# Gate and up of two of four batches by seven products of quarters

## The reference

```python
x = _layernorm(x + attention(x, Wqkv, bqkv, Wo, bo))          # 16 heads of 32
x = _layernorm(x + _wkv(w, u, x, ctx))                        # recurrence over the 512 tokens, per channel
Wg, Wu, Wd = dequant(gate_w), dequant(up_w), dequant(down_w)  # (w - 128) * scale per row; 2048x512, 2048x512, 512x2048
x = _layernorm(x + (silu(x @ Wg.T) * (x @ Wu.T)) @ Wd.T)
```

## Time and profile before

| | us |
|---|---|
| median of 3 runs (lowest, highest) | 726.25 (724.97, 728.55) |
| the profiled execution: its own time | 728.07 |
| its span, first to last instruction | 726.0 |
| busy: PE / DVE / ACT / POOL | 707.3 / 510.8 / 409.0 / 303.2 |

### The profile page before, as it was taken

One profiled execution on the slowest core, in us unless ns is written; L12 is line 12 of the kernel. 1 busy time (PEld: TensorE's weight loads), 2 busy tenths in 40 slices (PEclk: granted clock), 3 DMA queues, 4 the chain that ended last, 5 costly groups with the idle time before them and its releaser, 6 DMA issues.

```text
span 726.0 us, 11976 instructions
## 1 busy us (share of the span) xinstructions
PE 707.3 (97%) x4274; PEld 391.4 (54%) x4274; DVE 510.8 (70%) x1191; ACT 409.0 (56%) x980; POOL 303.2 (42%) x338
## 2 busy tenths in 40 slices
PE   8898999999999999998999999999999999999997
PEld 3466665666665666666554445445544444544445
DVE  3588766799899889899826889866787734532224
ACT  5478877769886787679755662154612532133310
POOL 2016421464766314541356834474645733023310
PEclk9999999999999999999999999999999999999999
DMA  7728739344233234643044010000001000100001
GB/s 230 227 87 212 241 73 242 86 123 117 66 92 115 51 104 130 143 76 88 3 63 112 1 59 15 30 16 1 0 16 44 0 1 1 43 16 1 0 15 44
DMA packets 45530, 54.16 MB, mean 75 GB/s; under 512 B 4896, under 2 KB 34848, under 8 KB 45472
## 3 DMA queue, kind: packets, MB, share of 16 engines
q1 hardware_dynamic: 41632, 46.59, 21.9%
q0 software_dynamic: 3264, 6.29, 5.1%
q10 hardware_dynamic: 576, 0.52, 0.3%
HBM read 47.10 MB, written 12.58 MB: 82 GB/s over the span
## 4 chain that ended last, share of the span: by engine, by line
PE 87%; DVE 4%; ACT 3%; DMA 2%; issue 2%; SPq 1%; POOL 1%; ACTq 0%; POOLq 0%; DVEq 0%
PE psb L838 29%; PE psb L726 10%; PE psb L764 8%; PE psb L862 7%; PE psb L860 7%; PE psb L742 6%; PE psb L809 5%; PE psb L777 5%; PE psb L753 4%; PE psb L825 2%; PE psb L797 2%; PE psb L788 2%; DMA ks<-parts 1%; ACT ee L949 1%; DVE st L1143 1%
## 5 line engine op out<-in xcount | busy, mean ns | idle before, releaser
L1098 DVE CUSTOM_DVE_ANT_0 ee<-psb,mask,clip 128x512 f32<-128x512 f32 (+3 forms) x256 | 130.6, 535 | 20.7 <-PE psb L753 20.1
L949 ACT ACTIVATE ee<-ee,nm 128x512 f32<-128x512 f32 (+3 forms) x256 | 142.0, 559 | 1.5 <-DVE nm L1098 1.5
L1433 POOL TENSOR_TENSOR hl<-hf,hh 128x512 f16<-128x512 f32 x64 | 74.2, 1160 | 103.6 <-ACT hh L1024 103.6
L1024 ACT ACTIVATE hh<-hf 128x512 bf16<-128x512 f32 x64 | 40.3, 630 | 119.6 <-DVE hf L1222 115.1
L960 ACT ACTIVATE ee<-psb 128x256 f32<-128x256 f32 (+1 forms) x156 | 81.5, 531 | 42.7 <-PE psb L764 36.3
L764 PE MATMUL psb<-ident,ee 128*128 128x128 f32 x640 | 98.9, 274 | 3.3 <-DVE ee L1112 1.5
L1222 DVE SCALAR_TENSOR_TENSOR hf<-th,c,psb 128x512 f32<-128x512 f32 x60 | 43.7, 729 | 79.8 <-PE psb L838 63.2
L838 PE MATMUL psb<-x2h,wg 128*128 128x512 f16 x256 | 97.0, 379 | 0.0
L838 PE MATMUL psb<-x2h,wu 128*128 128x512 f16 x256 | 97.0, 379 | 0.0
L838 PE MATMUL psb<-x2l,wg 128*128 128x512 f16 x256 | 97.0, 379 | 0.0
L838 PE MATMUL psb<-x2l,wu 128*128 128x512 f16 x256 | 97.0, 379 | 0.0
(11 more groups left out here) (130 smaller groups left out, 1215.7 us busy)
## 6 DMA issues: line engine op xcount, KB each, us to landing
qs<-parts SPq DMA_DIRECT2D x64, 128.0 KB, 2.9
ks<-parts SPq DMA_DIRECT2D x60, 128.0 KB, 3.4
parts<-qhl SPq DMA_DIRECT2D x16, 256.0 KB, 2.1
parts<-khl SPq DMA_DIRECT2D x16, 256.0 KB, 2.3
x<-in_x SPq DMA_DIRECT2D x4, 1024.0 KB, 6.9
ct<-in_ctxT SPq DMA_DIRECT2D x4, 1024.0 KB, 5.3
out<-x SPq DMA_DIRECT2D x16, 256.0 KB, 2.0
xt<-in_xT SPq DMA_DIRECT2D x14, 256.0 KB, 4.2
```

The costliest lines, as they stand in the source:

```text
L949: e.activation(dst, dst, ACT.Exp, bias=NM[:, n % 4, col:col + 1], scale=-1.0, accum_out=DEN[:, n % 4, col:col + 1]).then_inc(sem("exp"), 1)
L1098: e.tensor_tensor_reduce(E[H % 3][:, EOFF[i]:EOFF[i] + w], PSB[:, bank["score", H, i], 0:w], MASK[:, S - w:S], -SC, CLIP[:, i:i + 1], ALU. ...
L1433: e.tensor_tensor(HS[it][1][:], ring(b, it)[1][:], HS[it][0][:], ALU.subtract).then_inc(sem("hl"), 1)
```

## The change

Gate and up of a batch are one product of two by two blocks: rows gate and up, channels in halves, tokens in halves. For batches 2 and 3 (`SEVEN`) its eight block products become seven products of sums (the scheme of Strassen and Winograd). A pair m is two hidden tiles, 2m and 2m+1; a product P1 to P7 is 8 matmuls of 256 columns, (2 tiles) x (2 tiles of channels) x (high, low). What goes into it are blocks or sums of blocks of the weights (`WSUM`, four sums of two pieces each, made once) and of the tokens (`x_sum`, made per batch).

- PE, pair m: P1, P5, P2, P6, P3, P4 of pair m-1, P7. P6, P4 and P7 add on to the bank sa that holds P1; P3 adds on to the bank of P5. P6 waits for ScalarE's copy snap1 of P1, P3 for snap5 of P5, P7 for snap6 of P1+P6, P4 for c22.
- VectorE: c11 and c12 write the two token halves of gate to SBUF, c22 the second half of up; hfa and hfb are the two halves of hf, for each tile. The order is c11(m), c12(m), hfa(m-1) twice, c22(m), hfb(m) twice.
- ScalarE: snap1, snap5, snap6, two Silu (in SBUF, behind c12), two hh of pair m-1. GpSimd: two hl as before. `WS_POOL`, `HFB_POOL` and `XLO_POOL` are all zero, so all sums are VectorE's.
- Ahead of a batch: x2t is copied whole (xf), VectorE makes four token sums (xt, 512 columns each), ScalarE four high parts (xhi) and VectorE four low parts (xlo), of 1024, 1024, 1024 and 512 columns.
- The eight weight sums (128x2048, f16) stand at slots 272 to 295.
- The recurrence of batch 3 is placed at 280, 289, 291, 296 (before: 288, 292, 294, 297), its yt at 301, 301, 304, 306 (302, 303, 303, 308), its x2t at 312 (314). Batch 2's x2t stand at 292 (290, 291, 291, 292). Nearly all other slots, of attention too, and the tables `TURN`, `OH_POOL`, `XH_POOL`, `COPIES`, `KEYS` are set anew; of these only a few are shown.

```diff
-W_SPLIT = (6, 7, 8, 11)
+W_SPLIT = (8, 9, 18, 20)
...
-WKV_AT = {(0, 0): 111, (0, 1): 123, (0, 2): 133, (0, 3): 143, (1, 0): 191, (1, 1): 209, (1, 2): 262, (1, 3): 264,
-          (2, 0): 266, (2, 1): 272, (2, 2): 274, (2, 3): 277, (3, 0): 288, (3, 1): 292, (3, 2): 294, (3, 3): 297}
-YT_AT = {0: (156, 164, 174, 183), 1: (269, 270, 270, 270), 2: (283, 283, 286, 287), 3: (302, 303, 303, 308)}
-X2_AT = {0: (225, 228, 230, 232), 1: (272, 272, 272, 273), 2: (290, 291, 291, 292), 3: (314, 314, 314, 314)}
+WKV_AT = {(0, 0): 111, (0, 1): 123, (0, 2): 134, (0, 3): 144, (1, 0): 193, (1, 1): 208, (1, 2): 262, (1, 3): 264,
+          (2, 0): 266, (2, 1): 272, (2, 2): 274, (2, 3): 277, (3, 0): 280, (3, 1): 289, (3, 2): 291, (3, 3): 296}
+YT_AT = {0: (158, 166, 167, 182), 1: (268, 269, 270, 270), 2: (283, 286, 287, 288), 3: (301, 301, 304, 306)}
+X2_AT = {0: (225, 226, 228, 230), 1: (272, 272, 272, 273), 2: (292, 292, 292, 292), 3: (312, 312, 312, 312)}
+WS_AT = {1: (272, 280), 2: (280, 284), 3: (277, 295), 4: (285, 291)}
...
+    def quarters(b, c):
+        add("xf", b, c)
+        if c == T - 1:
+            for k in range(4):
+                add("xhi", b, 0) if k == 0 else None
+                add("xt", b, k)
+                add("xhi", b, k) if k else None
+            for k in range(4):
+                add("xlo", b, k)
...
+    def seven_first(b, m):
+        if m == 0:
+            tt.flush(("xlo", b, 3))
+        for j, name in ((1, "sa"), (5, "sd"), (2, "sb"), (6, None)):
...
+            add("p", b, m, j)
+            if j == 2:
+                add("c11", b, m)
+            else:
+                add(f"snap{j}", b, m)
+
+    def seven_second(b, m):
+        for j in (3, 4, 7) if m < PAIRS - 1 else (4, 7, 3):
+            if j == 4:
+                fourth(b, m - 1)
+                continue
+            add("p", b, m, j)
+            if j == 3:
...
+                add("c12", b, m)
+            else:
+                add("c22", b, m)
+        for it in (2 * m, 2 * m + 1):
+            add("silu", b, it)
+        for it in (2 * m - 2, 2 * m - 1) if m else ():
+            add("hh", b, it)
+            add("hl", b, it)
+        for it in (2 * m, 2 * m + 1):
+            add("hfb", b, it)
...
-            gu(b, it)
+            if b in SEVEN:
+                (seven_second if it % 2 else seven_first)(b, it // 2)
+            else:
+                gu(b, it)
...
+        def product(b, m, j):
...
+            for k in (0, 1):
+                for kk in (0, 1):
+                    for low in (0, 1):
+                        mm = e.matmul(PSB[:, bk, k * HALF_S:(k + 1) * HALF_S], weights(j, kk, 2 * m + k),
+                                      moving(b, j, kk, low), start=(unit is not None and k + kk + low == 0),
+                                      stop=(kk + low == 2), skip_group_check=True)
+            mm.then_inc(sem("p"), 1)
...
+        def c12(b, m):
+            dve.wait_ge(*by_p(b, m, 3))
+            dve.wait_ge(*by("snap6", b, m))
+            e.tensor_tensor(pair(b, m)[:, :, HALF_S:S], PSB[:, bank["sd", b, m], :].rearrange("p (k n) -> p k n", k=2),
+                            SNAP2.rearrange("p (k n) -> p k n", k=2), ALU.add).then_inc(sem("summed"), 1)
```

More of the change, by code:

```diff
@@ L20 @@
 EPS = 1e-5
+HALF_S = S // 2
 EOFF = {0: 0, 1: 128, 2: 384, 3: 768}
@@ L44 @@
 OHS = 6
+SEVEN = (2, 3)
+PAIRS = IT // 2
+SIGNAL = {"snap1": "snap", "snap5": "snap", "snap6": "snap", "c11": "summed", "c12": "summed", "c22": "summed"}
+PART_READ = {1: 1, 2: 0, 3: 0, 4: 3, 5: 1, 6: 2, 7: 2}
 EARLY = 4
-W_SPLIT = (6, 7, 8, 11)
[L50 to L53, removed]
@@ L61 @@
 LAST_AT = (5, 5, 6)
[L62 to L68, removed]
@@ L79 @@
-X2_AT = {0: (225, 228, 230, 232), 1: (272, 272, 272, 273), 2: (290, 291, 291, 292), 3: (314, 314, 314, 314)}
[L80 to L90, removed]
+WAIT = {'high': 1, 'low': 1, 'vtake': 1, 'r1': 2, 'norm': 6, 'exp': 4, 'eb': 0, 't1': 1, 't3': 0, 'oh': 3, 'ol': 3,
+        'ek': 1, 'scan_q': 2, 'scan_p': 6, 'divide': 8, 'r2': 3, 'x2h': 1, 'x2l': 2, 'expand': 0}
@@ new lines @@
+WAIT_IN = {'r1': 0, 'norm': 2, 'ek': 0, 'scan_q': 1, 'scan_p': 1, 'divide': 2, 'r2': 0, 'x2h': 0, 'x2l': 3}
+PIECE_AT = {'load_second': 34, 'small': 86, 'split_wo': 46, 'load_ds': 186}
+WU_AT = (36, 49, 52, 57)
+WU_ZERO = (55, 123, 127, 150)
+WG_AT = (212, 214, 221, 229)
+WG_ZERO = (223, 230, 238, 241)
+REST_AT = (0, 31, 98, 20)
+BO_AT = (46, 102, 131, 180)
+XLOAD = {1: (1, 12, 23, 29), 2: (50, 60, 78, 80), 3: (129, 140, 153, 164)}
+XSPLIT = {1: (19, 25, 36, 37), 2: (88, 91, 96, 101), 3: (146, 156, 160, 165)}
@@ L159 @@
     "yt": lambda b, t: ("r2", b, t),
-    "x2t": lambda b, c: ("x2l", b, c),
+    "x2t": lambda b, c: ("xf" if b in SEVEN else "x2l", b, c),
+    "sa": lambda b, m: ("hfa", b, 2 * m + 1),
+    "sb": lambda b, m: ("c11", b, m),
+    "sd": lambda b, m: ("c12", b, m),
     "gate": lambda b, it: ("aa" if early(b, it) else "th", b, it),
@@ L433, in timetable @@
         piece(max(BO_AT[b], PIECE_AT["split_wo"] + 2), "add_bo", b)
+    for j, slots in WS_AT.items():
+        for kk, slot in enumerate(slots):
+            piece(slot, "ws", j, kk)
     for which, slot in WKV_AT.items():
@@ L699, in stacked, with weight_sum, x_part_low, hf_half @@
                 SCR[n, "qk".index(kind)][part].rearrange("(h p) t -> p h t", p=32))
+    def weight_sum(e, q, j, kk):
+        a, c, op = {1: (wu[:, kk, :], wu[:, 2 + kk, :], ALU.add), 2: (WSUM[1][kk], wg[:, kk, :], ALU.subtract),
+                    3: (wg[:, kk, :], wu[:, kk, :], ALU.subtract),
+                    4: (wg[:, 2 + kk, :], WSUM[2][kk], ALU.subtract)}[j]
+        q.wait_ge(*by("wo", B - 1, T - 1))
+        if j == 4:
+            q.wait_ge(sem("out0"), 16 * T)
+        if j in (2, 4):
+            q.wait_ge(*by_ws(j // 2, kk))
+        e.tensor_tensor(WSUM[j][kk], a, c, op).then_inc(sem(f"ws{j}"), 1)
+    def x_part_low(e, q, b, k):
+        src, high, dst = token_part(b, k)
+        q.wait_ge(*by("xhi", b, k))
+        e.tensor_tensor(dst, src, high, ALU.subtract).then_inc(sem("xlo"), 1)
+    def hf_half(e, q, b, it, first):
+        m, k = divmod(it, 2)
+        cut = slice(0, HALF_S) if first else slice(HALF_S, S)
+        at = pair(b, m)[:, k, cut]
+        q.wait_ge(*by("silu", b, it))
+        if first:
+            q.wait_ge(*by_p(b, m, 4))
+            up = PSB[:, bank["sa", b, m], k * HALF_S:(k + 1) * HALF_S]
+        else:
+            q.wait_ge(*by("c22", b, m))
+            up = SNAP5[m % 2][:, k * HALF_S:(k + 1) * HALF_S]
+        e.scalar_tensor_tensor(out=at, in0=at, scalar=C2[:, it:it + 1], in1=up, op0=ALU.mult,
+                               op1=ALU.mult).then_inc(sem("hfa" if first else "hfb"), 1)
     block = ctx.enter_context(nc.Block())
@@ L1066, in _ @@
                 th(*a)
+            elif name == "xf":
+                x_full(*a)
+            elif name == "xhi":
+                x_part_high(*a)
+            elif name in ("snap1", "snap5", "snap6"):
+                snap(*a, int(name[-1]))
+            elif name == "silu":
+                silu(*a)
+            elif name == "hh" and a[0] in SEVEN:
+                hh_seven(*a)
             elif name == "hh":
@@ L1322, in _ @@
                 hf(*a)
+            elif name == "ws" and not WS_POOL[a[0] - 1]:
+                weight_sum(e, dve, *a)
+            elif name == "xt":
+                x_sum(*a)
+            elif name == "xlo" and not XLO_POOL[a[0]]:
+                x_part_low(e, dve, *a)
+            elif name == "c11":
+                c11(*a)
+            elif name == "c12":
+                c12(*a)
+            elif name == "c22":
+                c22(*a)
+            elif name == "hfa":
+                hf_half(e, dve, *a, True)
+            elif name == "hfb" and not HFB_POOL[a[0]]:
+                hf_half(e, dve, *a, False)
             elif name == "yd":
@@ L1474, in _ @@
                 hl(*a)
+            elif name == "ws" and WS_POOL[a[0] - 1]:
+                weight_sum(e, pool, *a)
+            elif name == "xlo" and XLO_POOL[a[0]]:
+                x_part_low(e, pool, *a)
+            elif name == "hfb" and HFB_POOL[a[0]]:
+                hf_half(e, pool, *a, False)
     @block.sync
```

212 lines of the change are left out of this document (191 added, 21 removed).

## The result

The changed kernel takes 730.19 us (median of 4 runs, 729.65 to 730.49), the kernel before 725.61 beside it (724.90 to 728.55): ratio 1.0052, 95% interval 1.0027 to 1.0078. It is slower, where 720.7 was forecast. The two profiled executions took 729.65 and 728.07 (spans 727.9 and 726.0): the profile of before is an execution near the slow end of its kernel's times (the slowest took 728.55), that of after the fastest of its four, so the profiles show only 1.9 of the 4.6 us.

What follows compares the result with a forecast made beforehand. Behind 462 us the number of TensorE's matmul columns was taken to set the end. The terms 12.7 - 3.4 - 1.5 - 1.5 - 0.7 gave 5.6 us gained, from 726.25 to 720.7 us; range 713.5 to 729.

Steps and rivals of the forecast that it cites:

- Fewer columns: Gate and up of batches 2 and 3: 16 pairs at 6.12 us instead of 6.91 save 12.7 us.
- A clean pair costs nothing: Pairs without inserted work, all of batch 3: other engines fit within 6.12 us, margin 0.1 to 0.6 us, no TensorE wait.
- The chain of token sums is covered: Ahead of a batch: token sums and high/low parts, some 10 to 12 us, hidden behind three y totalling 20.7 us.
- Column (3,3): Batch 3's last recurrence column, inside batch 2's pair 0: P6 of pair 1 makes TensorE wait 3.4 us.
- The reciprocals: Column (3,3)'s four reciprocals in batch 2's pair 1: 3.7 us against 2.2 free on VectorE, costing 1.5 us.
- Residual steps and norm: Four r2 steps and the norm on VectorE in batch 2: 0.3, 0.1, 0.4 and 0.7, together 1.5 us lost.
- New work ahead of the batches: Weight sums at 0.91 us each, six in batch 1: fuller VectorE queue and a late first sum cost 0.7 us.
- Placements in the attention stage: New slots in the attention stage: costed at nothing, with 1.5 us kept either way for them and the moved DMAs.
- C: Rival, batch 2: GpSimd's hl holds up both hfb on the port shared with VectorE; slower, 731.7 us; chance 0.15.
- B: Rival, batch 1: weight sums take 2.29 us and overfill VectorE, 3.4 us more late, 724.1 us; chance 0.18.

Runs made afterwards that it cites:

- run without sums: Changed kernel with the eight weight sums left out, products reading plain weights instead: 727.57 us, ratio 1.0016 to the kernel before.
- early-table run: Changed kernel with one small unused Silu on ScalarE right behind column (3,3)'s exponentials: 729.69 us, ratio 1.0049 to the kernel before.
- slots-only run: Changed kernel's slots and tables, but no batch by seven products and no weight sums: 728.70 us, ratio 1.0023 to the kernel before.

## Why the prediction was wrong

- **Fewer columns, 12.7 us: right.** 0.109 us for a matmul of 256 columns, 49.0 us for a batch's eight pairs, at full clock.
- **A clean pair costs nothing: right.** Batch 3 has no wait. The half-wide product costs 0.476 on VectorE (0.47 forecast), the sums of 512 columns 0.68 to 0.69.
- **The chain of token sums is covered: right.** No P1 waited. In batch 3 it took 9.6 us, from the transposes at 623.2 to the end of the last low part at 632.8.
- **Column (3,3), 3.4 us: a step that failed; the wait was 5.7.** The run without sums has the forecast's times up to c12: ekv at 6.3 us into the batch (6.2 forecast), c12 at 10.2 (10.1). Two links behind it were wrong. I had no table load ahead of Silu; there is one, behind the wait for c12 and so in series, and the early-table run shows its price, 1.3 us. (The load that I had, ahead of the exponential, did not happen there; VectorE's queue took its place.) And I had P6 of pair 1 due at 9.2 us, with a whole pair of seven products before it; it was due at 8.3, because pair 0 has no P4 of a pair before it and so only six products, 0.9 us. 3.4 + 1.3 + 0.9 is 5.6. In the changed kernel ekv started at 8.1, since c11 stood behind VectorE's work for y(1,3) and the weight sum, but P6 was due later by the same 1.9 us, by which P7 had waited for that sum: that delay is paid at P7.
- **A term that was not there: the lower clock, 1.5 us** in the profiled execution (2.4 us in the early-table run). The wait was forecast, its effect on TensorE's clock was not.
- **The reciprocals, 1.5 us: right in size** (1.3 with the wait filled), but hidden at half clock in the changed kernel.
- **Residual steps and norm, 1.5 us: 2.3 measured**, in four waits in pairs 4 to 7. With hl cut 0.6 is left, so most of it hangs on the port.
- **New work ahead of the batches, 0.7 us: the term that was furthest off.** It was 1.9 us before P7 alone, and TensorE waited 3.6 us in batch 1, 5.5 together. I had added VectorE's work up over batch 1, 54 of 59.2 us (55.0 was measured), and found room. But the work is not spread: two sums of over 2 us each (489.16 and 491.14) stand right ahead of the early column (3,0)'s product and scans, and the 1.6 us wait follows at 496.3. Without sums 1.8 of the 3.6 us stay, and with the sums but the column at its old slot only 0.4, so the column costs 1.8 by itself and the sums cost theirs together with it. The sums took 1.16 to 1.29 us and twice over 2, not 0.91. By the Trainium skill (VectorE: DVE Perf Modes, The perf-mode tier table) the estimate was 1.2, and the trace agrees for the six that took 1.16 to 1.29.
- **Placements in the attention stage, nothing: wrong.** The slots-only run shows 2 to 3.6 us at like clock, 1.5 of it behind the attention stage, so 0.5 to 2 us are left for that stage.

The waits of the profiled execution are 3.6 + 1.9 + 5.7 + 1.5 + 2.3 = 15.0 us, against 7.1 forecast, and against a gain of 12.7: 2.3 us lost, and the two traces show 2.2 from the start of batch 1's gate and up to the end (266.0 us against 263.8). The medians show 4.6. TensorE's clock in the first 30 us, before first,

```profile
0.00:30.00 30.00, 25.15 (x90) 9.81 (x91) 12.12 (x23) 13.71 (x24) 4.84 (x10) 0.89 0.76 224
```

```profile
0.00:30.00 30.00, 25.55 (x111) 11.12 (x112) 14.59 (x35) 17.44 (x35) 4.85 (x10) 1.00 0.85 246
```

was at its lower level in two spells in the profile of before and never in that of after, which is luck of the execution and hides part of the loss: executions of the kernel before at a mean clock of 0.998 or more have spans of 722.4 to 723.6 us, some 3 us below the profiled 726.0. The 2.3 us, with up to 2 us of the attention stage, come near the 4.6. That last share is an estimate from the slots-only run; two batches by seven products with the old attention tables were not run.

Of the rivals, C came nearest in time (731.7), but its mechanism carried 2.2 us and not 11. B's price (2.29 us for a sum) was wrong; its place, batch 1, was right. None of them had the table load, the six products of pair 0 or the clock.

## What to carry to other kernels

Where one engine has no gap, a change that saves its work by giving more to others should go where those have room: here it gained 6.3 us in the batch whose VectorE was a quarter busy and lost 5.0 us in the one that was 60% busy and had the recurrence's last column in its first pair, with 3.2 us more in the batch before that took the new work. Count a chain that the full engine will wait for link by link, with table loads in series and with the first round's own order of products, and add what the wait does to TensorE's clock.

## What the runs showed that was not expected

- Short idle spells of TensorE cost twice. After waits of 2.2 to 5.7 us the granted clock was at 1.2 GHz (0.54 of full over the 3.5 us behind the changed kernel's longest), and with 4.4 us of matmuls inside the same wait it stayed at 1.00. The Trainium skill (TensorE: Matmul & The Clock Gate, Part 1) says that idleness lowers the clock; the runs agree.
- A table load of 1.28 us stands behind the wait of the Silu that needs it (566.35, with c12 done at 566.27), though ScalarE had been idle for 7.28 us; the copies ahead of it brought no load. A small Silu ahead took it out of the chain (load at 559.79).
- Two-tensor instructions of VectorE in SBUF are held up by GpSimd: hfb 0.71 us with hl at 512 columns, 0.48 with hl at 8. A weight sum took 1.16 to 1.29 in six places and 2.05 and 2.18 in the two (489.16, 491.14) where GpSimd's hl and product ran beside it; hl took 2.13 there. The rule of the Trainium skill (SBUF — State Buffer, SBUF: two separate sides) agrees.
